# Two graph layers on one core: node rows prepared in 49 tiles over 128 partitions instead of 50 over 125, and the first chunk table taken off DRAM

## What is computed

```python
q, k, v = X @ Wq, X @ Wk, X @ Wv                   # 6250 x 128 each
scores = einsum('ehd,ehd->eh', q[dst], k[src]) / sqrt(16)
alpha  = softmax of scores over the edges of one dst
agg    = segment_sum(alpha[:, :, None] * v[src], dst)
h1 = layer_norm(X + agg @ W0)
x  = layernorm(X + layer_norm(h1 + relu(h1 @ fc1) @ fc2))
# layer 1
h_in  = segment_sum(relu([x[src], ea, req] @ W1f + b1f) @ W2f + b2f, dst)   # first half of the edges
h_out = the same with W1b, W2b                                               # second half
out = layernorm(x + relu(((1 + eps) * x + h_in + h_out) @ Wu + bu))
```

## Time and profile before

| | us |
|---|---|
| median of 3 runs | 2345.27 |
| the runs | 2341.87, 2346.10, 2345.27 |
| span of the profiled execution | 2343.1 |
| first gather of layer 0 (POOL L663) starts | 117.56 |
| last gather of layer 0 starts | 1102.7 |

### The profile page before, as it was taken

The page is one execution under the profiler, slowest core; times in us unless marked ns, Lnnn a source line. Parts: engine busy times, 40 slices in busy tenths (PEclk is TensorE's granted clock), DMA queues, the critical chain, the costliest instruction groups (busy, mean ns, idle before and its releaser), DMA issues.

```text
span 2343.1 us, 31906 instructions
## 1 busy us (share of the span) xinstructions
PE 1413.2 (60%) x7352; PEld 1104.8 (47%) x7353; DVE 1443.4 (62%) x2963; ACT 743.4 (32%) x1515; POOL 1594.1 (68%) x1668
## 2 busy tenths in 40 slices
PE   5234656555555556556688566666666666566665
PEld 3134655455455455555566444444444444344443
DVE  2246978877877777778477444554554554544544
ACT  2143434344344334334367311111111111111111
POOL 4077777777777777776433277777777777777774
PEclk9657877778777778777799777777777777777777
DMA  4478555555555555554000122222222222222221
GB/s 167 126 177 279 175 155 163 166 155 163 166 154 159 169 156 154 173 156 146 22 33 35 48 60 63 65 63 62 65 64 63 65 64 65 63 64 65 63 63 45
DMA packets 149172, 255.38 MB, mean 109 GB/s; under 512 B 74828, under 2 KB 100096, under 8 KB 149004
## 3 DMA queue, kind: packets, MB, share of 16 engines
q0 software_dynamic: 65072, 160.39, 24.2%
q1 hardware_dynamic: 82194, 92.81, 12.8%
q10 hardware_dynamic: 1870, 1.78, 0.2%
HBM read 233.19 MB, written 28.04 MB: 111 GB/s over the span
## 4 chain that ended last, share of the span: by engine, by line
POOL 60%; issue 22%; DMA 5%; DVE 5%; PE 4%; ACT 2%; POOLq 1%; another core or an unknown queue 1%; DVEq 0%; SPq 0%; ACTq 0%; PEldq 0%
POOL arena L720 31%; POOL arena L663 28%; DMA kvq_tab<-arena 3%; DMA arena<-kvq_tab,arena 1%; ACT arena L876 1%; PE ps L1083 1%; DVE arena L1526 1%; DMA xs<-in_x_dram 1%; DVE arena L1516 0%; PE ps L1119 0%; DVE arena L1471 0%; PE ps L1124 0%; PE ps L1171 0%; DVE arena L1551 0%
## 5 line engine op out<-in xcount | busy, mean ns | idle before, releaser
L663 POOL DMA_INDIRECT arena<-kvq_tab,arena x784 | 747.5, 953 | 265.9 <-issue 264.9
L720 POOL DMA_INDIRECT arena<-y_tab,arena x784 | 739.8, 944 | 252.4 <-issue 238.6
L1083 PE MATMUL ps<-arena 128*128 128x136 f32 x1568 | 316.1, 388 | 413.4 <-DVE arena L1471 413.4
L1083 PEld LDWEIGHTS ps<-arena 128*128 128x128 f32 x1568 | 306.4, 292 | 428.5 <-issue 428.5
L953 ACT ACTIVATE arena<-arena 128x512 f32<-128x512 f32 x224 | 123.3, 572 | 795.3 <-DVE arena L1607 795.3
L1607 DVE TENSOR_TENSOR arena<-ps,arena 128x512 f32<-128x512 f32 x224 | 134.7, 621 | 353.8 <-DMA arena<-y_tab,arena 344.6
L1233 PEld LDWEIGHTS ps<-arena 128*128 128x128 f32 x1568 | 265.1, 244 | 163.7 <-ACT arena L953 95.8
L1233 PE MATMUL ps<-arena 128*128 128x128 f32 x1568 | 286.4, 336 | 30.3 <-ACT arena L953 29.6
L1220 PE MATMUL ps<-w1blk,eaT 113*128 x456 | 253.3, 643 | 0.6 <-ACT eaT L948 0.6
L1417 DVE TENSOR_TENSOR arena<-ps,arena 128x512 f32<-128x512 f32 x224 | 137.9, 616 | 170.6 <-DMA arena<-kvq_tab,arena 168.5
L1059 PE MATMUL ps<-arena 128*128 128x128 f32 x1596 | 212.1, 287 | 41.7 <-ACT arena L812 26.8
(11 more groups left out here) (247 smaller groups left out, 1949.6 us busy)
## 6 DMA issues: line engine op xcount, KB each, us to landing
arena<-d SPq DMA_DIRECT2D x58, 897.0 KB, 4.9
arena<-kvq_tab,arena POOLq DMA_INDIRECT x784, 2.7
arena<-y_tab,arena POOLq DMA_INDIRECT x784, 2.5
arena<-ea SPq DMA_DIRECT2D x60, 112.0 KB, 2.0
ea<-in_edge_attr_dram SPq DMA_DIRECT2D x2, 3125.0 KB, 19.1
y_tab<-arena SPq DMA_DIRECT2D x10, 625.0 KB
kvq_tab<-arena SPq DMA_DIRECT2D x6, 937.5 KB
arena<-kvq_tab SPq DMA_DIRECT2D x59, 64.0 KB
```

The lines of the kernel that those rows point to most:

```text
L663: g.indirect_dma_start(kv_s[:, r, t, :], None, kvq_tab.rearrange("n (a d) -> (n a) d", a=3), bass.IndirectOffsetOnAxis(ap=v3(idx, RING)[:, ...
L720: g.indirect_dma_start(yg_s[:, r, t, :], None, y_tab, bass.IndirectOffsetOnAxis(ap=v3(idx1, RING)[:, r, t:t + 1], axis=0)).then_inc(m_g[r] ...
L1083: last = mm(sums, hot_s[:, u, t, :], contrib_s[:, u, t * RW:(t + 1) * RW], start=(t == 0), stop=(t == G - 1))
```

## The change

The preparation works on 49 tiles of 128 nodes (6272 rows, the last 22 of them zero) in seven groups of seven. Partition 127 has only 27 rows; DVE clears the rest first (`s_xz`). `x` comes in as 112 partitions in four DMAs, 15 partitions in two, and one partition in one. Three staging slots take the place of five, and all seven stores are SP's. The edge lists use 80 partitions with 625 entries instead of 125 with 400. The first node of each chunk is read from the input `dst` by ACT, in six small DMAs, onto one partition; PE spreads it over all partitions by a product with ones; DVE works out the first chunk table before it takes any product out of PSUM; PE turns it (`turn_table`), and DVE copies it to its places. Layer 1's table still goes by DRAM. The middle stage needs `x` in 125 partitions by 50 rows, so SP loads it again in `late_loads(0)`, inside layer 0's loop.

```diff
-EP, EQ = 125, 400
+EP, EQ = 80, 625
+PT, PG = 49, 7
+PGROUPS = PT // PG
+PN = P * PT
+WHOLE = 112
...
-        KVR = 5
-        BY_POOL = (2, 4, 6, 8)
+        KVR = 3
+        slots = [(i % KVR, i // KVR) for i in range(PGROUPS)]
...
@@ SyncE @@
-            for k in range(GROUPS // 2):
-                sp.dma_start(v3(xs[:, :], TILES)[0:NT, k * span:(k + 1) * span, :], x_rows[:, k * span:(k + 1) * span, :]).then_inc(s_x[k], 16)
-                if k == 0:
-                    sp.dma_start(v3(xs[:, :], TILES)[NT:P, :, :], x_rows[0:P - NT, :, :]).then_inc(s_xr, 16)
+            sp.dma_start(x3[0:WHOLE, 0:PG, :], x_rows[0:WHOLE, 0:PG, :]).then_inc(s_x[0], 16)
+            sp.dma_start(x3[WHOLE:FULL, 0:PG, :], x_rows[WHOLE:FULL, 0:PG, :]).then_inc(s_xb[0], 16)
+            sp.dma_start(x3[FULL:P, 0:LAST, :], x[FULL * PT:N, :].rearrange("(p t) d -> p t d", p=1)).then_inc(s_xb[0], 16)
+            sp.wait_ge(s_xz, 1)
+            sp.dma_start(x3[0:WHOLE, PG:3 * PG, :], x_rows[0:WHOLE, PG:3 * PG, :]).then_inc(s_x[1], 16)
+            sp.dma_start(x3[WHOLE:FULL, PG:PT, :], x_rows[WHOLE:FULL, PG:PT, :]).then_inc(s_xb[1], 16)
+            for k in (2, 3):
+                sp.dma_start(x3[0:WHOLE, (2 * k - 1) * PG:(2 * k + 1) * PG, :],
+                             x_rows[0:WHOLE, (2 * k - 1) * PG:(2 * k + 1) * PG, :]).then_inc(s_x[k], 16)
...
-                sp.dma_start(by_row(kvq_tab, i * GRP, GRP)[:, :, 0:QKV], kvst_s[0:NT, u, :, :]).then_inc(s_kvo[u], 16)
+                sp.dma_start(by_row(kvq_tab, i * PG, PG), kvst_s[:, u, :, :]).then_inc(s_kvo[u], 16)
...
-            for i in range(GROUPS):
-                if i not in BY_POOL:
-                    store_rows(i)
-            sp.wait_ge(s_tabi[0], 32)
+            for i in range(PGROUPS):
+                store_rows(i)
+            sp.wait_ge(s_tab0, 2)
...
                     sp.dma_start(ways, tbe[0:TE, 7:9]).then_inc(s_tabo, 16)
+                    node_rows = x.rearrange("(p t) d -> p t d", t=TILES)
+                    sp.dma_start(v3(xs[:, :], TILES)[0:NT, :, :], node_rows).then_inc(s_xr, 16)
+                    sp.dma_start(v3(xs[:, :], TILES)[NT:P, :, :], node_rows[0:P - NT, :, :]).then_inc(s_xr, 16)
@@ GpSimd @@
-            store_rows(2)
-            pool.wait_ge(s_d0, 48)
-            pool.dma_start(firsts[0].rearrange("(b c) -> b c", c=1), marks(d0[1:1 + NB * CH]), allow_slow_non_contiguous=True).then_inc(s_first[0], 16)
...
-            pool.dma_start(tabs[0], tbe[0:TE, 0:5].bitcast(I32)).then_inc(s_tabo[0], 16)
-            pool.dma_start(negs[0].rearrange("(p c) -> p c", c=1), tbe[0:TE, 5:6]).then_inc(s_tabo[0], 16)
-            store_rows(8)
...
-            pool.dma_start(tab_sb[0][:, :], tabs[0].rearrange("(a e) f -> a (e f)", a=1)).then_inc(s_tabi[0], 16)
-            pool.dma_start(nj[0][:, :], negs[0].rearrange("(a e) -> a e", a=1).to_broadcast([P, TE])).then_inc(s_tabi[0], 16)
@@ ScalarE @@
+            load_marks(0, 0, NB - 1)
+            load_mark(NB - 1, (NB - 1) * CH)
+            load_marks(NB, 0, BLK - 1)
+            load_mark(NB + BLK - 1, (BLK - 1) * CH)
+            load_marks(NB + BLK, HALF, BLK - 1)
+            load_mark(2 * NB - 1, HALF + (BLK - 1) * CH)
             act.dma_start(v3(dsti, 2)[0:EP], dst_halves).then_inc(s_dst, 16)
...
-                act.wait_ge(s_tabi[0], 32)
+                act.wait_ge(s_tab0, 2)
@@ TensorE @@
+            pe.wait_ge(s_markf, 1)
+            mm(bank(7)[:, 0:2 * NB], ones[0:1, :], markf).then_inc(s_markb, 1)
...
+            def turn_table():
+                pe.wait_ge(s_tab, 1)
+                for f in range(2):
+                    tp(bank(7)[0:1, (f + 1) * TE:(f + 2) * TE], tbe[0:TE, f:f + 1], ident[0:TE, 0:TE])
+                mm(bank(7)[:, 3 * TE:4 * TE], ones[0:TE, :], diag[0:TE, :]).then_inc(s_turn, 1)
...
-                    if j >= 6:
-                        pe.wait_ge(*((s_cv, vecs(j - 6)) if j % 2 else (s_ca, acts(j - 6))))
-                    mm(bank(2 + j % 6)[0:NT, 0:QKV], v3(xT, 2)[:, i % 2, t * P:t * P + NT], wqkv[:, :]).then_inc(s_kv, 1)
+                    if j >= 5:
+                        pe.wait_ge(*((s_ca, acts(j - 5)) if j % 2 else (s_cv, vecs(j - 5))))
+                    mm(bank(2 + j % 5)[:, 0:QKV], v3(xT, 2)[:, i % 2, t * P:(t + 1) * P], wqkv[:, :]).then_inc(s_kv, 1)
+                if i == 1:
+                    turn_table()
@@ VectorE @@
+            v.memset(v3(xs[:, 0:PT * D], PT)[96:P, LAST:PT, :], 0.0).then_inc(s_xz, 1)
             v.memset(ps[:, :], 0.0).then_inc(s_wq, 1)
+            dve.wait_ge(s_mark, 16 * 6)
+            v.tensor_copy(markf, marki).then_inc(s_markf, 1)
...
+            dve.wait_ge(s_markb, 1)
+            link(v.tensor_copy(markb, bank(7)[:, 0:2 * NB]))
+            chunk_table(0)
+            dve.wait_ge(s_dst, 32)
+            v.tensor_copy(dstf[0:EP], dsti[0:EP]).then_inc(s_pre, 1)
...
-                if i == 6:
-                    chunk_table(0)
+                if i == 2:
+                    dve.wait_ge(s_turn, 1)
+                    v.tensor_copy(tab_sb[0][0:1, 0:2 * TE], bank(7)[0:1, TE:3 * TE]).then_inc(s_tab0, 1)
+                    link(v.tensor_copy(nj[0][:, :], bank(7)[:, 3 * TE:4 * TE]))
+                    ts(njc[:, :], nj[0][:, :], iota_col[:, :], None, ALU.subtract).then_inc(s_tab0, 1)
```

More of the change, by code:

```diff
@@ L99, in gnn_kernel @@
         ea1 = dram("ea1", (ALL1, EA), F32)
-        firsts = [dram(f"first{l}", (NB,), F32) for l in range(2)]
-        tabs = [dram(f"tab{l}", (TE, 5), I32) for l in range(2)]
-        negs = [dram(f"neg{l}", (TE,), F32) for l in range(2)]
+        tab1 = dram("tab1", (TE, 5), I32)
+        neg1 = dram("neg1", (TE,), F32)
         ways = dram("ways", (TE, 2), F32)
@@ L184, in gnn_kernel @@
         assert top[0] <= hot0 + 2 * CH
-        xT = carve(2 * GRP * P, 0)
-        KVR = 5
-        BY_POOL = (2, 4, 6, 8)
-        slots = [(0, 0), (1, 0), (3, 0), (2, 0), (4, 0), (0, 1), (3, 1), (1, 1), (4, 1), (2, 1)]
-        kvst = carve(KVR * GRP * QKV)
+        xT = carve(2 * PG * P, 0)
+        KVR = 3
+        slots = [(i % KVR, i // KVR) for i in range(PGROUPS)]
+        uses = [len(range(k, PGROUPS, KVR)) for k in range(KVR)]
+        kvst = carve(KVR * PG * QKV)
         srci = carve(2 * EQ).bitcast(I32)
@@ L561, in _ @@
             g.memset(fill[0:1, :], -1.0).then_inc(s_pool, 1)
[L563 to L570, removed]
             row = lambda t: t.rearrange("(a n) -> a n", a=1)
-            marks = lambda a: a[0:NB * CH].rearrange("(b c) -> b c", c=CH)[:, 0:1]
             gap, tail = BASE1 - HALF, ALL1 - END1
-            spread = lambda l: pool.dma_start(first[:, 0:NB], firsts[l].rearrange("(a b) -> a b", a=1).to_broadcast([P, NB])).then_inc(s_first[l], 16)
             pool.wait_ge(s_pool, 3)
@@ L636, in _ @@
             pool.wait_ge(s_ea, 16 * 10)
-            pool.wait_ge(s_tabi[0], 32)
+            pool.wait_ge(s_tab0, 2)
+            pool.wait_ge(s_ca, acts(PT - 1))
+            pool.wait_ge(s_cv, vecs(PT - 1))
+            for k in range(KVR):
+                pool.wait_ge(s_kvo[k], 16 * uses[k])
             pool.sem_inc(s_init, 1)
@@ L736, in _, with load_marks, load_mark @@
             a = nc.scalar
+            def load_marks(at, start, n):
+                starts = dst[start:start + n * CH].rearrange("(b c) -> c b", c=CH)[0:1, :]
+                act.dma_start(marki[:, at:at + n], starts, allow_slow_non_contiguous=True).then_inc(s_mark, 16)
+            def load_mark(at, start):
+                act.dma_start(marki[:, at:at + 1], one(dst[start:start + 1])).then_inc(s_mark, 16)
+            load_marks(0, 0, NB - 1)
[4 more added lines that the diff above has]
+            load_mark(2 * NB - 1, HALF + (BLK - 1) * CH)
             act.dma_start(v3(dsti, 2)[0:EP], dst_halves).then_inc(s_dst, 16)
             act.dma_start(v3(srci, 2)[0:EP], src_halves).then_inc(s_dst, 16)
[L741 removed]
+            kvst_s = kvst.rearrange("p (u t d) -> p u t d", u=KVR, t=PG)
             def act_first(i):
                 act.wait_ge(s_xTp, i + 1)
[L745 removed]
+                a.activation(v3(xT, 2)[:, i % 2, :], bank(0, 2)[:, 0:PG * P], ACT.Copy).then_inc(s_xT, 1)
             act_first(0)
[L748 to L749 removed]
+            for i in range(PGROUPS):
+                if i + 1 < PGROUPS:
                     act_first(i + 1)
@@ L1345, in chunk_table @@
                 dve.sem_inc(s_tab, 1)
-            kvst_s = kvst.rearrange("p (u t d) -> p u t d", u=KVR, t=GRP)
-            dve.wait_ge(s_const, 5)
-            link(v.memset(tbe, 0.0))
-            dve.wait_ge(s_pool, 4)
-            for i in range(GROUPS):
+            dve.wait_ge(s_const, 6)
+            v.memset(tbe, 0.0)
+            dve.wait_ge(s_markb, 1)
[3 more added lines that the diff above has]
+            v.tensor_copy(dstf[0:EP], dsti[0:EP]).then_inc(s_pre, 1)
@@ new lines, in _ @@
+            ts(v3(srcb, 2)[0:EP, 0, :], v3(srci, 2)[0:EP, 0, :], 2.0, None, ALU.mult)
```

(7 more changed lines are left out.)

161 lines of the change are left out of this document (73 added, 88 removed).

## The result

The change made the program 17.5 us faster, not 48: the median is 2328.18 us against 2345.68, a ratio of 0.9925 with a 95% interval of 0.991 to 0.9939. I had forecast 2297, with a range from 2284 to 2316; the measured time lies above its upper end.

What follows compares the result with a forecast made beforehand. POOL's gathers in layer 0 were taken as the bound, movable by the first gather's start: 117.56 to 69.6 us, 48.0 earlier. Span 2343.1 - 48.0 = 2295.1, median 2.2 over it: 2297 us, range 2284 to 2316.

Steps and rivals of the forecast that it cites:

- What bounds the kernel: Layer 0's loop: 784 POOL gathers, 1.26 us each; only the first gather's start or a new gap moves its end.
- Five engines: Preparation: SP's or ACT's DMAs over 125 partitions use 5 of 16 engines (share 0.32); 112, 80 or 128 use 16.
- VectorE before its first copy: Start of preparation: clearing, chunk-start loads, first table and conversions put VectorE's first copy at 20.7 us, before 23.21.
- The marks: Preparation: ACT's six small loads of chunk starts, taken to land at 9.2 us, bounds 7.6 and 17.4.
- Products: PE in preparation: 43 tiles in 32.3 us, 1 for turning the table, 4 for half clock; last copy at 59.0.
- Stores and first gather: End of preparation: last store issued at 59.6, 4.2 us long, lands at 67.2; first gather 2.4 later, 69.6.
- The table without DRAM: Preparation: the first table skips three DRAM round trips; worth nothing by itself, ready by 40 us.
- The reload: Layer 0's loop: SP loads xs again, 3.2 MB, 27 us on five engines; costed at nothing, hidden by 20 us slack.
- second rival: Layer 0's loop, chunks 4 to 6: the reload opens about 19 us of gap; gain 29, 2316; chance 0.12.
- slow stores: Preparation's three store slots: DRAM writes limit stores to 29 us each, first gather at 232, total 2460; chance 0.03.
- no spread: Preparation's stores: 128 partitions stay on five engines, seven stores take 82 us; gain 6, 2339; chance 0.04.
- half clock: Preparation's products: PE at half clock throughout, 54.6 us, 18 later; gain 30, 2315; chance 0.12, shared with late marks.

Runs made afterwards that it cites:

- e1: The changed kernel, but only the last of the 50 tiles of xs is reloaded (0.07 MB instead of 3.3): 2300.04 us, ratio 0.9806.
- e5: The kernel of e1 with each of SP's seven stores split over 125 and 3 partitions: 2348.94 us, ratio 1.0008.
- e4: The kernel before the change with only the same reload of xs added at the same place: 2377.87 us, ratio 1.0133.
- e2: The changed kernel with SP's reload in three DMAs over 112, 13 and 3 partitions instead of 125 and 3: 2312.46 us, ratio 0.9864.
- e10: The changed kernel, reload by ACT in four parts, one per pass for chunks 0 to 3, each over 125 and 3 partitions: 2313.01 us.
- e3: The changed kernel with the same two reload DMAs (125 and 3 partitions) issued by ACT in its pass for chunk 0: 2322.79 us.

## Why the prediction was wrong

By its own steps:

- *What bounds the kernel.* Right. Layer 0's loop is POOL's row of gathers; the start of it moved the end wherever no gap came (e1: first gather 48.9 us earlier, total 45.6 us less).
- *Five engines.* Right, and shown both ways: the share of 0.94 after, and e5, where 125 partitions bring back 0.32 and the whole time. A store was even faster than estimated, 396 GB/s for 329.
- *VectorE before its first copy.* 26.07 instead of 20.7. The marks landed just before 12.33, not at 9.2 (ACT's first issue took 1.44 us, not 0.58), and the source indices only at 23.46; I had them landed by 17.4. By my own sign, a first copy past 25 us, the small loads would be the failed step; they are not, since the first gather still came in time.
- *Products.* 26.67 to 60.61 is 33.9 us for the 43 tiles, where I had 33.3 and 4 more for a lower clock. The granted clock was 0.50, the lower of its two levels, only from 28 to 30 us (0.70 in the two us before, 0.94 in the two after), behind PE's wait of 3.78 us for the first copy; from 32 to 61 us it was 1.00, with PE at work all the time. I had tied the 0.50 of the earlier trace rows to the time since PE's work began; it stood beside a pause too, of 10.28 us.
- *Stores and first gather.* Last store issued at 61.16, first gather at 68.80: 7.6 us where I had 10.0. The sum, 69.6 for 68.8, is right partly by luck: the late first copy (+5.4) is cancelled by the clock (about -3.4) and the stores (-2.4).
- *The table without DRAM.* Turning it took PE under 1 us, within what I had counted. By e5 it brings nothing while the stores are slow; whether it was needed once they were fast stays open.
- **The reload, "I cost it at nothing".** This is the step that failed, and what stood at nothing measured 28 us (e1), 32 in the old kernel (e4). It has two errors. I compared bytes, "the reload is half of that", with a copy that goes over all 16 engines. Over five, half the bytes load an engine 1.6 times as much, and its packets of 25.6 KB run from 110.0 to 151.9 us in the trace, 42 us and not 27, while gathers and SP's loads move on the same engines. And I took the slack as there for each disturbance anew. It is one stock, 20 us by my reckoning; the reload drew it down to nothing, it was not back when the edge copy started 26 us after the reload's last packet, and that copy, harmless before with 8.3 us left, cost 9.3 us in its turn. The same is seen in e2 (10.3), not in e1. In e10 (16.4) the fourth part of the reload goes out just behind the edge copy, so there the two also overlap. How fast the slack comes back was not measured.

My second rival had the place and two thirds of the price: 19 us of gap, 2316 in all, against 28 us and 2328. I gave it 0.12. What I wrote against it, that the first transfer is over when the second starts, was true of the transfers and not of the slack. Its mechanism was half of what happened: gathers that landed late made 5.4 us of gap; the larger gap came behind SP's loads, which went out up to 30 us late and then took 17 to 21 us to land. The prediction named those loads as queued behind the reload, and then gave them no price. The other rivals (slow stores, no spread, half clock) didn't come.

What stays open: how the 28 us divide between gathers and SP's loads in each case. e3 shows that both suffer even in separate queues, and no run takes one of the two victims away. Nor was it tried why an issue is held as long as it is, or whether the early table is needed beside the fast stores.

## To carry over

Before a transfer is called hidden, divide its bytes by the engines that it can use, not by 16, and ask which small loads that others wait for need the same engines. A slack in front of the bounding engine is one stock for all disturbances that come close together: two that each fit can cost when they meet. A late reload belongs over a number of partitions that fills the engines, and in parts, one per period of the loop; here that turned 17.5 us of gain into 42 to 48.

## What the hardware did that I had not expected

- The issue of one small DMA took 20.41 us on SP, and 31.81 in e3, where the large transfer stood in ACT's queue. So an engine's issues can be held while another engine's transfer fills five DMA engines.
- A pair of small loads landed in two parts: 22 of 32 rises of its semaphore came by 143.2 us, ten at 159.4 to 162.6, and VectorE went on at 162.7. So such a load is as late as the fullest of its engines makes it.
- Rows of 5.1 KB instead of 25.6 KB shortened that issue to 10.9 us but not the time (2322.44 against 2322.79), and held ACT, which issued the reload, for 23.2 us.
- ACT's load of 55 single values of `dst` took 1.44 us to issue, the two of 27 values 0.78 each, against 0.28 to 0.43 for a single value.
